# A two-layer decoder on one core: mixture of experts by sorted rows, in a stage of its own

## The reference

```
x = x + attention0(norm(x))            # 16 heads of 128, causal, biases
x = x + wkv(norm(x), ctx)              # exponential recurrence over 64 steps
x = x + moe(norm(x))                   # 16 experts + shared experts
x = x + attention1(norm(x))            # differential, rotary, filtered by a fixed circulant
x = x + cross1(norm(x), ctx)           # a summary of the context per sequence, norm, gamma, beta
x = x + ffn1(norm(x))                  # inputs and weights quantized to three values
```

## Time and profile before

| | us |
|---|---|
| median of 3 runs | 1496.78 |
| lowest, highest | 1495.08, 1497.60 |
| span of the profiled execution | 1493.4 |
| TensorE busy | 1294.4 (87%) |
| VectorE busy | 1019.2 (68%) |
| GpSimd busy | 545.2 (37%) |
| ScalarE busy | 451.1 (30%) |

### The profile page before, as it was taken

The page is one execution under the profiler, slowest core; times in us unless marked ns, Lnnn a source line. Parts: engine busy times, 40 slices in busy tenths (PEclk is TensorE's granted clock), DMA queues, the critical chain, the costliest instruction groups (busy, mean ns, idle before and its releaser), DMA issues.

```text
span 1493.4 us, 26550 instructions
## 1 busy us (share of the span) xinstructions
PE 1294.4 (87%) x9595; PEld 1139.5 (76%) x9650; DVE 1019.2 (68%) x2124; ACT 451.1 (30%) x890; POOL 545.2 (37%) x535
## 2 busy tenths in 40 slices
PE   6999999999999982597998988989999989899752
PEld 6888989888889871486887777877887878778531
DVE  5667766776676776555666877867767768677673
ACT  5433333333434320241232222322322323223120
POOL 1113121212213121121454644635536446355453
PEclk9999999999999996698999999999999999999975
DMA  6200100000000000652000000010000000000000
GB/s 192 72 15 1 30 1 29 0 28 0 28 28 0 22 1 22 184 158 74 1 2 15 1 16 15 0 29 0 0 29 0 14 15 0 21 1 1 14 1 21
DMA packets 30515, 40.36 MB, mean 27 GB/s; under 512 B 6434, under 2 KB 24194, under 8 KB 30306
## 3 DMA queue, kind: packets, MB, share of 16 engines
q1 hardware_dynamic: 30434, 39.39, 8.6%
HBM read 35.12 MB, written 4.26 MB: 26 GB/s over the span
## 4 chain that ended last, share of the span: by engine, by line
PE 30%; DVE 13%; issue 7%; POOL 7%; ACT 1%; DMA 1%; SPq 0%; DVEq 0%; POOLq 0%; ACTq 0%
PE b_p_acc L1422 7%; PE b_p_s L1476 3%; POOL b_work L1271 3%; PE b_p_g L1337 2%; PE b_p_g L1338 2%; PE b_p_g L1339 2%; PE b_p_u L1337 2%; PE b_p_u L1338 2%; PE b_p_u L1339 2%; DVE b_q_bd L1873 1%; PE b_p_s L1495 1%; POOL b_dif L1275 1%; DVE b_act_w L1822 1%; DVE b_rsm L1894 1%; PE b_p_c L1413 1%
## 5 line engine op out<-in xcount | busy, mean ns | idle before, releaser
L1313 POOL TENSOR_TENSOR b_act_w<-b_act_w,b_col_w 128x512 f32<-128x512 f32 (+1 forms) x104 | 129.6, 1246 | 293.4 <-DVE b_act_w L1826 163.0
L1422 PE MATMUL b_p_acc<-b_down,b_act_w 128*128 128x256 f32 x800 | 195.8, 387 | 12.8 <-POOL b_act_w L1313 12.8
L322 POOL TENSOR_TENSOR a_probs<-a_shifted,a_rowinv 64x512 f32<-64x512 f32 x64 | 71.0, 1110 | 314.8 <-DVE a_rowinv L729 312.2
L1422 PEld LDWEIGHTS b_p_acc<-b_down,b_act_w 128*128 128x128 f32 x800 | 146.5, 194 | 31.7 <-POOL b_act_w L1313 14.3
L575 ACT ACTIVATE a_qk<-a_p_proj,a_b_col 128x256 f32<-128x256 f32 x256 | 106.9, 470 | 204.5 <-PE a_p_proj L391 203.9
L389 PE MATMUL a_p_proj<-a_xt_hi,a_w_hi 128*128 128x256 f32 x512 | 149.2, 291 | 5.5 <-DVE a_w_lo L693 5.0
L1337 PE MATMUL b_p_g<-b_xt_hi,b_up_hi 128*128 128x256 f32 x400 | 139.8, 349 | 9.3 <-DVE b_act_w L1822 7.4
L390 PE MATMUL a_p_proj<-a_xt_lo,a_w_hi 128*128 128x256 f32 x512 | 143.3, 280 | 0.0
L391 PE MATMUL a_p_proj<-a_xt_hi,a_w_lo 128*128 128x256 f32 x512 | 143.1, 280 | 0.0
L1617 ACT ACTIVATE b_act_w<-b_p_g 128x512 f32<-128x512 f32 (+1 forms) x104 | 60.4, 581 | 254.4 <-PE b_p_g L1339 254.2
L1338 PE MATMUL b_p_g<-b_xt_lo,b_up_hi 128*128 128x256 f32 x400 | 117.3, 293 | 0.0
(11 more groups left out here) (254 smaller groups left out, 3342.6 us busy)
## 6 DMA issues: line engine op xcount, KB each, us to landing
a_terms<-w_qkv SPq DMA_DIRECT2D x12, 512.0 KB, 4.8
b_work<-w_up SPq DMA_DIRECT2D x12, 512.0 KB, 3.6
b_down<-w_down SPq DMA_DIRECT2D x12, 256.0 KB, 3.9
a_xin<-x SPq DMA_DIRECT2D x8, 256.0 KB, 3.0
a_terms<-w_o SPq DMA_DIRECT2D x4, 512.0 KB, 4.7
a_xres<-x SPq DMA_DIRECT2D x8, 256.0 KB, 2.8
a_vch<-ctx_ch SPq DMA_DIRECT2D x8, 256.0 KB, 2.9
x_mid<-a_x SPq DMA_DIRECT2D x8, 256.0 KB, 2.2
```

The lines of the kernel that those rows point to most:

```text
L322: pool.tensor_tensor(probs[r, :, SEQ * s:SEQ * s + SEQ], expd[r, :, :], rowinv[r, :].unsqueeze(2).broadcast_to([SEQ, TC * GH, SEQ]), ALU.m ...
L1313: pool.tensor_tensor(a, a, col_w[:, 0:w, :], ALU.mult).then_inc(S["a_done"], 1)
L1422: mm = nc.tensor.matmul(p_acc[:, c, :], act_w[:, p % 2, t, c * P:c * P + P], down[:, j, :], start=j == 0 and c == 0, stop=j == FT - 1, ski ...
```

## The change

One program takes the place of two. All tiles are placed by hand in one memory plan (`memory`), in which tiles of later stages lie over those of earlier ones, and there is no barrier; each stage is a set of functions per engine that are called one after the other.

In attention the loops over blocks are written out, and each block's gating moves in: with a lag of two blocks come a norm (`g_stats`, `g_apply`), a transpose, the gate matmul, the choice of experts (`g_top`) and the ranks of the tokens within each expert by matmuls with triangles of ones (`rank`, `g_slots`, `g_share`). GpSimd then scatters every token's normed row, with an id in a 257th column, to four places of a DRAM buffer `xs` with 2176 rows per expert: 8 indirect DMAs of 128 rows per block (`scatter`), each followed by a wait for its completion.

The expert stage has 112 steps of 128 rows: 32 for the shared expert in two halves of 176, and 80 for the tiles of the experts, a fixed number that holds every possible split. At each step `up` makes 352 columns in 6 split matmuls with the rows as the stationary side, `turn_act` transposes the 176 columns in two halves, and `low` applies the down projection. Which expert a tile belongs to is read at run time from a table (`value_load`). SP first writes a padding of 128 rows behind each expert's rows (`pad`), then loads each tile's rows by a start that it reads from the table. GpSimd scatters each result to `yt` by the ids that came with the rows (`store`). The weights of all experts are loaded after attention's last matmul, as their place is attention's until then, and split during the shared steps; the last block's wkv and the gating of the last two blocks run there, too, and so do the constants and the context's summary for layer 1.

Layer 1 follows as a stage of its own, with the same schedule and without experts. What is new in it is `comb`: it loads the four results of each token and adds them with their weights to x plus the shared part, for the next block in the rows 8 to 11 of the schedule.

```diff
+NCH = BATCH * SEQ // P
+NSH = 2 * NCH
+NTILE = BATCH * SEQ * TOPK // P + NEXP
+NSTEP = NSH + NTILE
+NSTG_E, NXE, NYS = 4, 4, 3
+A_PIECES, A_CONST, A_SET = 16, 5, 12
...
+        def scatter(b, n):
+            c, k = n // TOPK, n % TOPK
+            if n == 0:
+                pool.wait_ge(slots_ready, b + 1)
+            if b == 0 and n == 0:
+                pool.wait_ge(d_gate, 16 * 6)
+            done = TC * TOPK * b + n
+            pool.tensor_copy(xg[:, b % 2, c, DIM:DIM + 1].bitcast(mybir.dt.int32),
+                             ids[:, TC * b + c, k:k + 1]).then_inc(id_set, 1)
+            pool.wait_ge(id_set, done + 1)
+            pool.indirect_dma_start(
+                out=xs, out_offset=bass.IndirectOffsetOnAxis(ap=slot[:, TC * b + c, k:k + 1], axis=0),
+                in_=xg[:, b % 2, c, :], in_offset=None).then_inc(d_scat, 16)
+            pool.wait_ge(d_scat, 16 * (done + 1))
...
+        def body(i, first, last):
+            if not first:
+                k_rstd(i - 1)
+            if not last:
+                norm_rstd(i + 1)
+            residual(i)
+            for j in range(NGRP):
+                b = i - 2 if j == NGRP - 1 else i - 3
+                n = 2 * ((j + 1) % NGRP)
+                if j < NGRP - 1 and b >= 0:
+                    scatter(b, n)
+                if not (last and j == NGRP - 1):
                     scale_probs(NGRP * i + j + 1)
-                    if j == 1 and not first:
-                        weigh(i - 1)
-
-            norm_rstd(0)
-            pool.wait_ge(d_const, 16 * 5)
-            scale_probs(0)
-            body(0, True, False)
-            body(1, False, False)
-            with pool.Fori(2, LAST) as i:
-                body(i, False, False)
-            body(LAST, False, True)
...
+            wait(dve, d_mid, 16 * i)
+            wait(dve, g_norm, i)
+            nc.vector.tensor_tensor(x1[:, :, :], p_out[:, :, :], xres[:, :, :], ALU.add
+                                    ).then_inc(x1_ready, 1)
...
+                if j == 1 and i >= 2:
+                    g_top(i - 2)
+                if j == 3 and i >= 2:
+                    g_share(i - 2)
+                if j == 3 and not first:
+                    wkv_add(i - 1)
+                    g_stats(i - 1)
+                    g_apply(i - 1)
+                if first and j == NGRP - 1:
+                    reset_columns()
+                    time_weights()
+            take_out(i)
...
+        def rows(r):
+            q = NCH + r
+            wait(sp, et_split, q - NXE + 1)
+            wait(sp, id_taken, r - NXE + 1)
+            if r == 0:
+                sp.wait_ge(A["d_zero"], 16 * (1 + TOPK + NEXP))
+            first = sp.value_load(tab[r:r + 1, 0:1], min_val=0, max_val=NEXP * ROWS_X + 1)
+            sp.dma_start(xe[:, q % NXE, :], xs[bass.ds(first, P), :]).then_inc(d_e[q % NXE], 16)
+        def pad(e):
+            if e == 0:
+                sp.wait_ge(A["tab_ready"], 3)
+                sp.wait_ge(A["d_scat"], 16 * NBLK * TC * TOPK)
+            first = sp.value_load(fill_i[0:1, e:e + 1], min_val=0, max_val=NEXP * ROWS_X + 1 - P)
...
+            if s == NSH - 4:
+                for n in range(NEXP):
+                    pad(n)
+                for r in range(3):
+                    rows(r)
...
+                e = experts_of[r] = pe.value_load(tab[r:r + 1, 1:2], min_val=0, max_val=NEXP - 1)
+                w_hi, w_lo = (t[:, bass.ds(e, 1)].rearrange("p a k d -> p (a k) d") for t in (up_hi, up_lo))
+            for k in range(KC):
+                mm = split3(p_gu[s % 2][:, 0:2 * IEXP], et_hi[:, q % 2, k * P:k * P + P],
+                            et_lo[:, q % 2, k * P:k * P + P], w_hi[:, k, :], w_lo[:, k, :],
+                            k == 0, k == KC - 1)
+            mm.then_inc(up_done, 1)
...
+        for s in range(NSTEP + 2):
+            if s < NSTEP:
+                up(s)
+            if NSH <= s + 2 < NSTEP:
+                turn(source(s + 2))
+            if 1 <= s < NSTEP + 1:
+                turn_act(s - 1)
+            if s >= 2:
+                low(s - 2)
...
+                wait(dve, d_y, 16 * (r - NYS + 1))
+                nc.vector.tensor_copy(y_sb[:, r % NYS, :], p_y[:, 0:DIM]).then_inc(y_out, 1)
...
+        def take_id(r):
+            q = NCH + r
+            pool.wait_ge(d_e[q % NXE], 16 * (q // NXE + 1))
+            pool.tensor_copy(idt[:, r:r + 1], xe[:, q % NXE, DIM:DIM + 1].bitcast(mybir.dt.int32)
+                             ).then_inc(id_taken, 1)
+        def store(r):
+            pool.wait_ge(y_out, r + 1)
+            pool.wait_ge(id_taken, r + 1)
+            pool.indirect_dma_start(
+                out=yt, out_offset=bass.IndirectOffsetOnAxis(ap=idt[:, r:r + 1], axis=0),
+                in_=y_sb[:, r % NYS, :], in_offset=None).then_inc(d_y, 16)
+            pool.wait_ge(d_y, 16 * (r + 1))
+        for r in range(NTILE + 5):
+            if r < NTILE:
+                take_id(r)
+            if r >= 5:
+                store(r - 5)
...
+        def comb(b, k):
+            if k == 0:
+                dve.wait_ge(S["d_x3"], 16 * (b + 1))
+                dve.wait_ge(S["d_g"], 16 * (b + 1))
+                if b == 0:
+                    dve.wait_ge(A["share_ready"], NBLK)
+                chains["m"] = Chain(dve, A["ln_chain"], b, M_STEPS, 4 * NBLK)
+            ch = chains["m"]
+            for c in range(TC):
+                ins = nc.vector.scalar_tensor_tensor(
+                    x3[:, b % 2, c, :], yg[:, c, k, :], share[:, TC * b + c, k:k + 1],
+                    x3[:, b % 2, c, :], ALU.mult, ALU.add)
+                if c == 0:
+                    ch.also(ins)
+                elif k < TOPK - 1:
+                    ch(ins)
+            if k == TOPK - 1:
...
+        def y_load(b):
+            wait(sp, S["x3_ready"], b)
+            sp.dma_start(yg[:, :, :, :], yt_blk[b]).then_inc(S["d_g"], 16)
```

3575 lines of the change are left out of this document (1914 added, 1661 removed).

## The result

The changed kernel takes 1672.03 us (median of 4 runs, 1669.92 to 1673.66), against 1495.93 (1494.69 to 1497.60) for the kernel before on the same chip: a ratio of 1.118, 95% interval 1.1162 to 1.1194. It is slower by about 12%. The profiled execution spans 1671.1 us.

The account below looks back on a forecast made before the run. TensorE was taken to pace both stages of the kernel before. For the changed one, attention 621 + expert stage 466 + layer 1 592 = 1679 us of span, with 3.4 around it 1683 us; 8-in-10 range 1500 to 1790.

Parts of the forecast that it names:

- Layer 1 alone: Layer 1 without experts to fill it, a chain of hand-overs: 72.2 us a block, 592 us in all.
- The tiles: 80 expert tiles at the pace of GpSimd's scatter and landing wait: 3.9 us each, 312 us.
- rival C: Expert stage at its engines' pace, scatters wholly hidden, no hole before the first tile: 1440 us, faster; chance 0.11.
- The scatter in attention: GpSimd's scatter of 128 rows in attention, with id copy and wait for landing: 3.9 us each.
- The 12 us that slot 0 was to lose: Attention, slot 0: a scatter before `scale_probs` makes the probabilities 2.4 us late, in 5 blocks 12 us.
- The 20 us at the joint: Attention, slot 3: `g_rstd` behind two scatters delays `g_apply` and `take_out`, 4 us in each of 5 blocks.
- The 12 us for `g_top`: Attention, slot 2: VectorE's `g_top` chain before the copy of transposed probabilities costs 2 us a block, 12 us in all.
- TensorE's added work: Attention: added transposes, gate and rank matmuls cost TensorE 1.5 us a block, 9 us in all.
- TensorE's 290 us removed: TensorE's expert work: about 290 us less, a gain only if nothing else sets the pace.
- Between attention and the first tile: Expert stage up to its first expert tile: 145 us, with TensorE empty for some 35 of them.
- A: Cheap scatters: 2.5 us each, landing and copy alone, tiles at 2.6 us, 1547 us in all; chance 0.22.
- B: Dear scatters: 5.5 us each, as VectorE and GpSimd hinder each other, 1847 us in all; chance 0.13.

Follow-up runs that it names:

- 6: Changed kernel with layer 1's next-block norm and transposes moved beside this block's pow, and the combining two schedule rows earlier: 1647.2 us, ratio 1.1010.
- 12: From 11, the root of layer 1's inner norm, with its squares and sums, taken in two halves of the heads: 1483.1 us, ratio 0.9899.
- 3: Changed kernel with three result stores in flight, GpSimd not waiting for its own landing in the first 64 of 80 tiles: 1579.7 us, ratio 1.0547.
- 2: Changed kernel with TensorE's gating transpose placed behind the first two projections of slot 0 instead of ahead of them: 1662.5 us, ratio 1.1110.
- 5: Changed kernel with the gating norm moved from the block's end to slot 0 of the next, its transpose behind the scores, `g_top` cut in two: 1643.4 us.
- 1: Changed kernel with every scatter of the attention stage issued and waited for twice: 1725.2 us, ratio 1.1538.
- 4: Changed kernel with three paddings before the first tile instead of sixteen, the others each just ahead of its tile's rows: 1674.6 us, ratio 1.1182.
- 7: Changed kernel with the last block's wkv and gating earlier, its last 13 scatters two in flight, six paddings before the rows: 1665.4 us, ratio 1.1130.
- 8: Changed kernel with 3 (for all 80 tiles), 5, 6 and 7 together: 1508.3 us, ratio 1.0079.
- 9: From 8, all sixteen paddings at shared step 22 on SyncE, first three tiles' rows at steps 26 to 28: 1506.8 us, ratio 1.0062.
- 11: From 9, the paddings issued by GpSimd behind its own last scatter instead of by SyncE: 1500.4 us, ratio 1.0023.

## Why the prediction was right, and which of its steps were not

The forecast was 1683 us and 1672.0 were measured, in the range, and slower as forecast. The mechanism holds: removing matmuls from a TensorE that had been busy nine tenths gives nothing back where the stages no longer share an engine's time. What ran woven together in 99.6 us a block now lies end to end, expert work at 3.70 us a tile and layer 1 at 72.4 us a block, and neither is bound by TensorE. The stages come out as forecast within 10 us each, partly by errors that cancel: that attention came within 5 us is in part luck, as its four terms did not come as they were set (below).

**Layer 1 alone: right.** 72.41 us a block against the 72.2 taken from the last block of the kernel before. That one stretch in the earlier trace rows carried 592 us of the sum; it measured the stage before it existed. That the block is a chain, not work, is shown by 6 and 12: 4.3 us a block gained by moving a norm beside the pow and the combining two rows up, 2.0 by halving the pow and what leads to it, with no work removed. The combining did cost nothing, as forecast. The bounds by the clock were not needed: it was granted 0.71 in that block, as in the earlier trace rows 0.72.

**The tiles: pace right, its parts not.** 3.9 us were forecast as landing 2.2, pass over the rows 1.28, copy 0.26, hand-over 0.16. The rows of the middle of the stage give issue 0.98, landing 1.9, copy 0.18, hand-over of the id 0.52, in all 3.6. That GpSimd's round of store and wait is everybody's pace is shown by 3 (3.70 to 2.27 without the wait). TensorE's pace behind it was mis-sized, 1.9 for 2.27. Between 922.02 and 924.29 in 3, the second of the six `up` matmuls starts 0.36 behind the first and not 0.16, and the four of `low` take 0.67 and not 0.48; the rest is as forecast. For rival C, whose point of decision was 2.75 us for each of 112 steps, this alone is 80 x 0.37 = 30 us more.

**The scatter in attention: price too high, cause wrong.** A scatter there takes 3.0 us with its copy (issue 1.0, landing 1.5), for a forecast of 3.9; the estimate of 2.6 us from the Trainium skill ("DMA: Bandwidth & Descriptors", Anatomy of one DMA), its 2.3 and the id copy, is nearer than mine, and still 0.4 low. In the stretch in which the experts' weights are loaded it takes up to 6.5 us (4.53 us of it the wait for the landing at 726.69). The 12 us that slot 0 was to lose to it fell away. GpSimd does wait there for the landing ahead of `scale_probs`, in 5 blocks, as forecast; but TensorE comes to the probabilities later itself, being held at the joint before, and waits 0.2 us in all. In 2, where it is held for less, 4.9 us of that wait appear: one delay had hidden the other, where the forecast added them. The 20 us at the joint did come (17.3 in L617's waits), but not from two scatters of slot 3: the pow came 2 us late in the forecast because of them, and here they have landed some 0.4 us before the statistics that it also needs, as one takes 3.0 us and not 3.9. The joint at 177.73 has no scatter ahead of it and costs 2.18 us already; what comes on top is as long as the shares on VectorE. What costs there is one more norm (statistics on VectorE, pow on GpSimd, apply on VectorE) right where the block ends, with `take_out` and TensorE's first gating transpose behind it. 5 takes it from there and gains 28.6 us with every scatter kept; 1 doubles the scatters and shows how far they are hidden. The 12 us for `g_top` are there, as 10.8 us of waits for `pt`.

**TensorE's added work: mis-sized.** 1.5 us a block were forecast. From one `take_out` to the next TensorE is busy 67.46 us, against 65.06 in the kernel before: 2.4 more, each with one drop of the clock in it (0.98 in both). The block of 5 with 65.42 has no such drop; one of its later blocks that has one (381.67 to 452.85) comes to 67.32. In all, a middle block grew by 6 to 7 us (from 68.3 to 68.6 up to 74.3 to 75.0), where the terms of the forecast add up to 9.9 (1.5, 2, 2.4 and 4). The prediction took 66.6 us for a block; its sum does not rest on this, as it starts from the whole stage's 568.3.

**TensorE's 290 us removed.** They were never a term of the sum, only the gain that would stand if nothing else set the pace. TensorE's busy time fell by 111. Layer 1's matmuls now run at 0.71 of the clock, as against 0.97 when they were woven into the experts, and gating and transposes were added; what each has of the difference, no run separates.

**Between attention and the first tile: right in each part.** The last slots were known at 700.4, 83.5 us after attention (forecast 87), the scatters ended at 733 (116, forecast 118), 16 paddings took 17.1 us (forecast 16), TensorE stood empty for 28 us (forecast 35), and the first tile began after 143.8 us (forecast 145). 4, 7, 8 and 9 show that this time is hard to take away: what leaves the hole stands in front of something else in SyncE's order. GpSimd, idle at that point, was the place for the paddings (11).

**The rivals.** A, 2.5 us a store, was right on the bare scatter without load (issue 0.98, landing 1.53) and wrong on the loop around it, which has the id copy and its hand-over too. B's 5.5 us is met only by single scatters in the stretch in which the weights are loaded. The mechanism that it rested on, GpSimd and VectorE hindering each other, is there, but small: once in each of the blocks with eight scatters one stands beside VectorE's scans of the wkv, and its id copy takes 1.01 us instead of 0.18 and its issue 1.71 instead of 1.0 (299.90 and 301.19, 374.54 and 375.83). GpSimd's issue of an indirect DMA took 0.96 to 1.21 us in the tiles and at most 1.80 anywhere. The Trainium skill, cited beside it ("SBUF — State Buffer", the second heading on bandwidth pools), has a DMA from GpSimd grow from 620 ns to 3100 beside a VectorE copy in its two-port mode. No issue of these 144 grew so; but no run shows whether an operation beside them was in that mode, nor whether the longest landings (3.3 and 4.5 us) come from VectorE or from the loads, so the rule is neither borne out nor refuted here. C (1440) needs what the changed kernel does not have; with all of it that I found, the runs come to 1483.

## What to carry to other kernels

Before a phase is unwoven to save work on the busiest engine, look for a stretch in which one part already runs alone: its length times its count is the price of the new stage, and here a block of it was known to 0.3%. A loop in which an engine issues a DMA and waits for its own landing goes no faster than issue, landing and what stands behind the wait together (3.70 us here, where the other engines could do 2.27); give each buffer a semaphore of its own, give padding rows separate places to land, and where a wait must stay, put it ahead of the next issue (2.75). Compare blocks from one joint to the next: a window cut to the mean length is not a block. At the joint of two pipelined blocks an added hand-over can be paid in full, however small its operations are (0.9 us more on VectorE, 0.9 us more of an empty TensorE), so put a new norm where its engine's results are not the next thing wanted.
